# Two-layer decoder with experts: the expert weights' 16-bit halves prepared in an earlier phase, queries and keys saved in stacked order, another slot table for the routing

## The reference, cut to what matters

```python
x = x + L0_attn(ln(x))            # 16 heads of 16, full softmax, weights sign(W) * mean|W|
x = x + L0_xattn(ln(x), ctx)      # one head of 256, 64 context rows
x = x + L0_ffn(ln(x))             # ternary weights, 8-bit activations, 256 -> 1024 -> 256
x = x + L1_attn(ln(x))            # 16 heads: 4 causal, 12 causal with a window of 64
x = x + L1_xattn(ln(x), ctx, ctx) # 16 heads over 64 context rows
x = x + L1_ffn(ln(x)):            # 8 experts, the best 2 of each token, and a shared one
    shared = (silu(x @ sg.T) * (x @ su.T)) @ sd.T
    probs = sigmoid(x @ router.T + bias); top_p, top_i = top_k(probs, 2); top_p /= sum(top_p)
    for each expert e: y_e = (silu(x @ wg[e].T) * (x @ wu[e].T)) @ wd[e].T
    out = shared + sum over the two chosen of top_p * y_e
```

## Time and profile before

| | us |
|---|---|
| median of 3 runs | 2143.51 (2140.32 to 2156.59) |
| the profiled execution's own time | 2145.49 |
| its span, first to last instruction | 2143.4 |
| TensorE busy | 1688.7 (79%) |
| DVE / ACT / GpSimd busy | 1316.8 / 1118.9 / 979.4 |
| mean granted clock of TensorE | 0.889 |
| layer 0 attention | 0 to 586 |
| layer 0 cross-attention and feed-forward | 586 to 847 |
| layer 1 attention | 847 to 1352 |
| layer 1 cross-attention | 1352 to 1582 |
| experts: routing and shared expert | 1582 to 1762 |
| experts: blocks and end | 1762 to 2143 |

### The profile page before, as it was taken

One profiled execution on the slowest core, in us unless ns is written; L12 is line 12 of the kernel. 1 busy time (PEld: TensorE's weight loads), 2 busy tenths in 40 slices (PEclk: granted clock), 3 DMA queues, 4 the chain that ended last, 5 costly groups with the idle time before them and its releaser, 6 DMA issues. The chain is left out here.

```text
span 2143.4 us, 36053 instructions
## 1 busy us (share of the span) xinstructions
PE 1688.7 (79%) x12334; PEld 859.7 (40%) x12350; DVE 1316.8 (61%) x3599; ACT 1118.9 (52%) x1534; POOL 979.4 (46%) x987
## 2 busy tenths in 40 slices
PE   4888888888688887477777776577747779999997
PEld 2122222222245455123333333344424446666664
DVE  2666777777157897246666664455448865555555
ACT  2366676676445796245555554255446634444442
POOL 3144554541347630456777766255327751212222
PEclk8588999999789999669999988699968889999999
DMA  5331334330040000333333320322224432222216
GB/s 102 65 58 36 62 65 65 61 50 1 5 122 1 1 1 5 52 53 51 54 53 53 58 41 11 84 53 58 47 88 133 132 126 54 61 62 62 58 41 245
DMA packets 114435, 130.26 MB, mean 61 GB/s; under 512 B 22108, under 2 KB 98908, under 8 KB 114108
## 3 DMA queue, kind: packets, MB, share of 16 engines
q1 hardware_dynamic: 107780, 109.74, 25.0%
q0 software_dynamic: 6480, 18.23, 2.2%
HBM read 79.25 MB, written 47.55 MB: 59 GB/s over the span
## 5 line engine op out<-in xcount | busy, mean ns | idle before, releaser
L653 ACT ACTIVATE at_pexp<-ps 128x1024 f32<-128x1024 f32 (+3 forms) x480 | 385.8, 826 | 194.3 <-PE ps L890 193.1
L714 DVE TENSOR_REDUCE at_mx<-ps 128x1 f32<-128x512 f32 x512 | 324.2, 684 | 146.9 <-PE ps L897 144.9
L897 PE MATMUL ps<-at_ks,at_qs 48*128 48x512 f16 (+3 forms) x1024 | 288.7, 357 | 91.6 <-DVE at_mx L714 42.4
L161 PE MATMUL ps<-mo_wall,mo_xt 128*128 x1704 | 301.5, 327 | 1.0 <-DVE mo_xt L2540 0.5
L890 PE MATMUL ps<-at_qs,at_ks 50*128 50x512 f16 (+4 forms) x1024 | 249.7, 341 | 27.7 <-DMA at_qs<-at_mhl 23.1
L950 PE MATMUL ps<-at_pexp,at_vaug 128*32 128x512 f32 (+4 forms) x2048 | 223.4, 529 | 13.9 <-issue 11.2
L161 PEld LDWEIGHTS ps<-mo_wall,mo_xt 128*128 128x128 f16 x1704 | 161.2, 98 | 94.6 <-issue 3.5
L2304 POOL DMA_INDIRECT mo_yd<-mo_xn,mo_idu x71 | 68.1, 959 | 275.8 <-DVE mo_xn L2561 267.0
L716 DVE CUSTOM_DVE_ANT_0 at_junk<-ps,at_lmask 128x192 bf16<-128x192 f32 x384 | 115.5, 353 | 78.7 <-PE ps L897 77.5
L897 PEld LDWEIGHTS ps<-at_ks,at_qs 48*128 48x128 f16 x1024 | 75.6, 98 | 206.1 <-DVE at_mx L714 122.6
L2364 ACT ACTIVATE mo_sg<-ps 128x512 f32<-128x512 f32 x71 | 42.4, 597 | 186.9 <-PE ps L161 186.9
(11 more groups left out here) (396 smaller groups left out, 3853.2 us busy)
## 6 DMA issues: line engine op xcount, KB each, us to landing
at_qs<-at_scratch SPq DMA_DIRECT2D x96, 128.0 KB, 7.2
at_ks<-at_scratch SPq DMA_DIRECT2D x96, 128.0 KB, 7.8
mo_xw<-mo_xs SPq DMA_DIRECT2D x71, 136.0 KB, 2.4
at_scratch<-at_qkh SPq DMA_DIRECT2D x64, 128.0 KB, 1.8
at_scratch<-at_qkl SPq DMA_DIRECT2D x64, 128.0 KB, 1.8
mo_wall<-mo_yd SPq DMA_DIRECT2D x16, 512.0 KB, 10.8
x_qs<-x_queries SPq DMA_DIRECT2D x48, 128.0 KB
mo_stage<-in_m_gate SPq DMA_DIRECT2D x9, 512.0 KB, 3.9
```

The lines of the kernel that those rows point to most:

```text
L161: last = nc.tensor.matmul(out, lhs, rhs, start=(n == 0), stop=(n == len(terms) - 1))
L653: last = act.activation(columns(pexp[:, U % 2, hh], at, n, stride, width), columns(banks(r, ST[S % 2], 2), at, n, stride, width), ACT.Exp, ...
L714: last = ve.reduce_max(out, score, AX.X)
L897: return nc.tensor.matmul(banks(r, MX[i % 2])[:, piece.at:piece.at + piece.n], qs[rows, (n // 2) % 2, h // 2, piece.idx * P:(piece.idx + 1 ...
```

## The change

1. In layer 0 attention the side task grows from 12 chunks to 66: behind the 12 of `wlin` come 54 of the expert weights (9 experts x 3 matrices x 2 halves, 256 KB each). There are nine chunks per batch, at slots 1, 3, 5, 14, 15, 17, 28, 29 and 31 modulo 32. SP issues the load at the chunk's slot (behind the rows, saves, stack and x load of that slot), GpSimd does its three instructions one slot later, and SP stores the float16 halves (256 KB) to a DRAM tensor `moe_weights` four slots later.
2. `experts_phase` no longer loads float32 weights and no longer splits them. SP issues one DMA of 1.5 MB for the shared expert at the start and eight of 1.5 MB for the experts, each when the next batch's x is turned; the padding writes stand directly behind them.
3. `save` writes to DRAM in stacked order: three DMAs per piece in place of two (the half that the stack holds twice is written twice). `stack` then needs four DMAs of 48 partitions x 8 KB in place of twelve of 16 partitions. In layer 1 cross-attention it is six saves of 128 KB and two stack DMAs per batch.
4. `ROUTE` and `SHARED` get other slots, with the same periods; `SPLIT` goes.

```diff
+CHUNK_AT = (1, 3, 5, 14, 15, 17, 28, 29, 31)
+CHUNK_DO = (1, 1, 1, 4)
...
+            whalves = sb("whalves", [P, 2, 2, WCHUNK], F16)
...
-        scratch = nc.dram_tensor(f"{tag}_scratch", (nb, 2, P, 4, T), F16, kind="Internal").ap()
+        scratch = nc.dram_tensor(f"{tag}_scratch", (nb, 2, 2, 3 * DH, NP_, T), F16, kind="Internal").ap()
...
+        MOE_CHUNKS = 6 * (E_ + 1)
+        CHUNKS = LIN_CHUNKS + MOE_CHUNKS
+        def chunk_at(i):
+            return CHUNK_AT[i % len(CHUNK_AT)] + K * (i // len(CHUNK_AT))
...
             def save(b, m):
-                to = scratch[b] if b < nb else r.x1_queries[b - nb]
+                of_k, par = divmod(m, 2)
+                to = scratch[b, of_k, par] if b < nb else r.x1_queries[b - nb, par]
                 sp.wait_ge(qkh_ready, qk_before(b) + m + 1)
-                sp.dma_start(to[0, :, m, :], qkh[:, m, :]).then_inc(saved, 16)
+                for rep in (0, 1 + of_k):
+                    sp.dma_start(to[rep * DH:(rep + 1) * DH].rearrange("d i t -> i d t"), qkh[:, m, :]).then_inc(saved, 16)
                 sp.wait_ge(qkl_ready, qk_before(b) + m + 1)
-                sp.dma_start(to[1, :, m, :], qkl[:, m, :]).then_inc(saved, 16)
+                rep = 2 - of_k
+                sp.dma_start(to[rep * DH:(rep + 1) * DH].rearrange("d i t -> i d t"), qkl[:, m, :]).then_inc(saved, 16)
...
                 for par in range(2):
-                    for rep, (qpart, kpart) in enumerate(((0, 0), (0, 1), (1, 0))):
-                        rows = slice(64 * par + 16 * rep, 64 * par + 16 * rep + 16)
-                        sp.dma_start(qs[rows, p], scratch[b, qpart, :, par, :].rearrange("(i d) t -> d i t", d=DH)).then_inc(stacked, 16)
-                        sp.dma_start(ks[rows, p], scratch[b, kpart, :, 2 + par, :].rearrange("(i d) t -> d i t", d=DH)).then_inc(stacked, 16)
+                    rows = slice(64 * par, 64 * par + 3 * DH)
+                    for of_k, to in enumerate((qs, ks)):
+                        sp.dma_start(to[rows, p].rearrange("p i t -> p (i t)"), scratch[b, of_k, par].rearrange("p i t -> p (i t)")).then_inc(stacked, 16)
...
+            def keep_halves(j):
+                s, n, half = moe_chunk(j)
+                sp.wait_ge(lin_done, 2 * (LIN_CHUNKS + j + 1))
+                at = n * NW + half * WCHUNK
+                sp.dma_start(r.moe_weights[s, :, :, at:at + WCHUNK], whalves[:, j % 2]).then_inc(halves_out[j % 2], 16)
...
-                if binary and t >= 0 and t % (K // 2) == 4 and t // (K // 2) < LIN_CHUNKS:
-                    load_lin(t // (K // 2))
+                if binary:
+                    for i in chunks(t):
+                        load_lin(i)
+                    for i in chunks(t - CHUNK_DO[3]):
+                        if i >= LIN_CHUNKS:
+                            keep_halves(i - LIN_CHUNKS)
...
-                if binary and t >= K // 2 and t % (K // 2) == 4 and t // (K // 2) - 1 < LIN_CHUNKS:
-                    split_lin(t // (K // 2) - 1)
+                if binary:
+                    for i in chunks(t - CHUNK_DO[0]):
+                        scale_chunk(i)
+                    for i in chunks(t - CHUNK_DO[1]):
+                        chunk_high(i)
+                    for i in chunks(t - CHUNK_DO[2]):
+                        chunk_low(i)
...
-            for t in range(START, END):
-                for s, n in due(t, "LOAD"):
-                    load_weights(s, n)
-
+            sp.dma_start(sh[:].rearrange("p q n w -> p (q n w)"), r.moe_weights[0].rearrange("p q w -> p (q w)")).then_inc(sh_in, 16)
+            for e in range(E):
+                sp.wait_ge(xt_ready, 2 * (e + 1))
+                sp.dma_start(wall[:, e * EW:(e + 1) * EW], r.moe_weights[1 + e].rearrange("p q w -> p (q w)")).then_inc(wall_in, 16)
...
-ROUTE = {"STAT": -22, "RSTD": -17, "APPLY": -10, "HIGH": -10, "LOW": 2, "TURN": (-9, 6), "XT": (-3, 12), "LG": 6, "LOGITS": 17, "SIG": 16,
-         "CHOOSE": 20, "RANK": 18, "SLOTS": 27, "SCAT": (28, 30, 33, 49, 49, 49, 50, 51)}
+ROUTE = {"STAT": -22, "RSTD": -15, "APPLY": -11, "HIGH": -6, "LOW": 2, "TURN": (-14, 2), "XT": (0, 11), "LG": 3, "LOGITS": 16, "SIG": 18, "CHOOSE": 23,
+         "RANK": 16, "SLOTS": 28, "SCAT": (30, 31, 34, 43, 45, 46, 46, 49)}
-SHARED = {"GU": (11, 12, 41, 45), "SQ": (22, 33, 48, 50), "H": (26, 42, 49, 56), "HH": (38, 47, 48, 62), "HL": (43, 50, 66, 70), "PROJ": (64, 66),
-          "UPD": (77, 97)}
+SHARED = {"GU": (8, 9, 34, 41), "SQ": (27, 36, 47, 53), "H": (28, 38, 54, 56), "HH": (40, 40, 60, 63), "HL": (36, 47, 55, 56), "PROJ": (63, 65),
+          "UPD": (85, 99)}
-SPLIT = {"LOAD": (-105, -83, -71), "WHI": (-58, -42, -34), "WLO": (-42, -28, -19)}
-SPLIT_PERIOD = 35
```

More of the change, by code:

```diff
@@ L289, in attention_phase @@
             wstage = sb("wstage", [P, 2, WCHUNK])
+            whalves = sb("whalves", [P, 2, 2, WCHUNK], F16)
+            halves_out = [sem(f"halves_out{i}") for i in range(2)]
             x_in = [sem(f"x_in{b}") for b in range(nb)]
@@ L354, in attention_phase, with chunks, moe_chunk @@
         LIN_CHUNKS = NC * NLIN // WCHUNK
+        MOE_CHUNKS = 6 * (E_ + 1)
+        CHUNKS = LIN_CHUNKS + MOE_CHUNKS
+        def chunk_at(i):
+            return CHUNK_AT[i % len(CHUNK_AT)] + K * (i // len(CHUNK_AT))
+        def chunks(t):
+            return [i for i in range(CHUNKS) if chunk_at(i) == t]
+        def moe_chunk(j):
+            return j // 6, j % 6 // 2, j % 2
         def main_at(t):
@@ L439, in _ @@
                         load_x(b + 1)
-                if binary and t >= 0 and t % (K // 2) == 4 and t // (K // 2) < LIN_CHUNKS:
-                    load_lin(t // (K // 2))
+                if binary:
[5 more added lines that the diff above has]
+            if binary:
+                for i in range(2):
+                    sp.wait_ge(halves_out[i], 16 * MOE_CHUNKS // 2)
             if ahead:
-                sp.wait_ge(saved, 32 * qk_before(all_nb))
+                sp.wait_ge(saved, 48 * qk_before(all_nb))
         @block.gpsimd
@@ L1741, in save, with to @@
                 sp.wait_ge(q_ready, NC * (f + 1))
-                sp.dma_start(r.x1_queries[p, 0], qh[:]).then_inc(saved, 16)
+                def to(par, rep):
+                    return r.x1_queries[p, par, rep * DH:(rep + 1) * DH].rearrange("d i t -> i d t")
+                for par in range(2):
+                    for rep in range(2):
+                        sp.dma_start(to(par, rep), qh[:, par, :]).then_inc(saved, 16)
                 sp.wait_ge(ql_ready, f + 1)
-                sp.dma_start(r.x1_queries[p, 1], ql[:]).then_inc(saved, 16)
+                for par in range(2):
+                    sp.dma_start(to(par, 2), ql[:, par, :]).then_inc(saved, 16)
             def stack(b):
@@ L1755, in stack @@
                 if b >= AHEAD:
-                    sp.wait_ge(saved, 32 * (b - AHEAD + 1))
-                for rep, part in enumerate((0, 0, 1)):
-                    for par in range(2):
-                        at = 64 * par + 16 * rep
-                        sp.dma_start(qs[at:at + 16, p], r.x1_queries[p, part][:, par, :].rearrange("(i d) t -> d i t", d=DH)).then_inc(stacked[p], 16)
+                    sp.wait_ge(saved, 96 * (b - AHEAD + 1))
+                for par in range(2):
+                    sp.dma_start(qs[64 * par:64 * par + 3 * DH, p].rearrange("p i t -> p (i t)"), r.x1_queries[p, par].rearrange("p i t -> p (i t)")).then_inc(stacked[p], 16)
             def rows(b):
@@ L2311, in _ @@
         def _(act):
-            def split(s, n):
-                act.wait_ge(w_in[n], 16 * (s + 1))
-                act.activation(part_of(s, 0)[:, n * NW:(n + 1) * NW], stage[:, n, :], ACT.Copy, scale=WS).then_inc(w_hi, 1)
             def high(b):
@@ L2358, in _ @@
                     sigmoid(b)
-                for s, n in due(t, "WHI"):
-                    split(s, n)
             def block_squash(k):
@@ L2400, in settle @@
                 ve.wait_ge(step, steps.n)
-            def split(s, n):
-                ve.wait_ge(w_hi, 3 * s + n + 1)
-                part = slice(n * NW, (n + 1) * NW)
-                ve.scalar_tensor_tensor(out=part_of(s, 1)[:, part], in0=stage[:, n, :], scalar=WS, in1=part_of(s, 0)[:, part],
-                                        op0=ALU.mult, op1=ALU.subtract).then_inc(w_lo, 1)
             def apply(b):
@@ L2534, in _ @@
                         update(b, half).then_inc(x_done, 1)
-                for s, n in due(t, "WLO"):
-                    split(s, n)
             def block_in(k):
@@ L2669, in project @@
                     pe.wait_ge(y_ready, NK)
-                else:
+                elif b:
                     pe.wait_ge(x_done, 2 * (b - 1) + half + 1)
```

71 lines of the change are left out of this document (39 added, 32 removed).

## The result

The changed kernel takes 2168.9 us (median of 12 runs, 2157.2 to 2173.8) against 2142.6 us: ratio 1.0112, 95% interval 1.009 to 1.0133. The interval lies clear of 1: the kernel is slower by some 24 us by the ratio, 26 by the medians. Forecast was 2126, within 2090 to 2162. Its profiled execution spans 2169.6 us, 26.2 more than before.

The account below looks back on a forecast made before the run. TensorE was taken to set layer 0's pace, DVE to be routing's nearest bound. From 2145.5 us, experts -31.5, stacks -12.7 and layer 0 +25 gave 2126.3, so 2126, within 2090 to 2162.

Parts of the forecast that it names:

- Layer 0: Layer 0 attention: 54 more chunks on GpSimd make the split of the maxima late, +25 us, bounds 0 to +55.
- That is 2.1 late at best ... Sum 4.4 us late: Layer 0, slot 28 to the slot-11 split: 2.1 us late, +2 behind the stack, +0.3 for loads under chunks.
- Six batches have such a stretch; the last has no stack in it (2.5): Layer 0 count of late stretches: five at 4.4 us plus a last at 2.5, 24.5 us, taken as +25.
- Stacks: First stacks of three attention phases: four 48-partition DMAs at 170 GB/s come sooner, -12.7 us, from -2 to -22.
- that comes back, with the time to its last issue: Awaited first stacks: 4.6 us less transfer plus issue time saved; layer 0 -5.7, layer 1 -5, cross-attention only -2.
- Experts: Routing part of the experts: float32 loads and splits go, gaining at start, middle and end, -31.5 us in sum.
- Start: Routing start: without old splits and their waits, statistics follow the router at once, -6.5 us, between -3 and -7.
- end: Routing end: pads no longer stand behind the last weight load, so sorted rows are read sooner, -7 us, -4 to -10.
- The middle: Routing window: 22 DVE splits, 27.9 us, go; DVE 85% busy, so two thirds are gained, -18 us.
- New slots at nothing: Routing tables: new slots issue the same work in another order and cost nothing beyond the other terms.
- The third: Rival in layer 0: GpSimd becomes the bound behind stacks still at 113 GB/s, +55, total 2167 us; chance 0.13.
- The first: Rival in layer 0: the chunks fit GpSimd's idle time, costing 5 us or less, total 2104 us; chance 0.25.

Follow-up runs that it names:

- loads-ahead side task: Changed kernel with the chunks' loads and stores moved ahead of saves and stack on SP, one chunk of nine moved on GpSimd: 2126.9 us, ratio 0.9941 to the kernel before.

## Why the prediction was wrong

**What bounds the kernel** was right for layer 0: the split of the maxima is TensorE's wait, and GpSimd's busy share says little.

**Layer 0, +25 forecast, +49.6 measured in the wait.** The step that failed is "That is 2.1 late at best ... Sum 4.4 us late", and the count behind it. The mechanism was right, its size was half of what came. The fifth stretch, which has no load of x, is 7.3 late:
- the first chunk starts 426.60 - 416.25 = 10.35 us after the split at slot 28, not 398.2 - 389.3 = 8.9: its load is issued 0.3 us later, behind the third save, and lands after 3.8 us for 2.7. +1.4;
- a chunk back to back is 2.97, not 2.87: +0.6 for six;
- the wait behind the stack is 3.0, not 2: +1.0. The 0.3 for two waits did not come.

With 4.4 these give 7.1. Where x is loaded, SP issues 512 KB ahead of the chunk, which the prediction left out though it named SP's queue: 2 us more of idle, some 1.5 of lateness.

"Six batches have such a stretch; the last has no stack in it (2.5)" is a miscount. Seven stretches hold six chunks, and six of them have a stack; the seventh, without one, costs nothing in the wait. From split to split the six are 2.8, 8.7, 9.0, 8.9, 7.3 and 11.2 us longer than before, together 226.6 - 178.8 = 48 us, for 5 x 4.4 + 2.5. The average, 8.0, lies in the range given for a stretch, 0 to 9, and the last lies outside it. Nearly all of these errors had the same sign: it was a sum of things that just fit, and where a chain has no slack, an omitted term only makes it longer.

**Stacks, -12.7 forecast, -7.3 at the three starts** (-3.4, -3.0 and -0.9 where TensorE resumes, against the phase's start). The rate was nearly right, 162 GB/s over the 8 us that the stack of layer 1 fills, up to 172, for the 170 taken:

```profile
931.00:933.00 2.00, 0.00 (x0) 0.00 (x0) 0.00 (x0) 0.00 (x0) 1.86 (x2) 0.83 1.11 172
931.00:939.00 8.00, 1.03 (x8) 0.77 (x8) 0.00 (x0) 1.02 (x1) 4.20 (x3) 0.58 1.03 162
```

What failed is "that comes back, with the time to its last issue": in layer 1 the stack went from issue to TensorE in 11.8 us for 15.5, 3.7 less, so the issues had been under the transfer; and it starts 0.7 us later, since SP waits 2.3 us for the last save's landing, where before it waited 1.4.

An estimate from the Trainium skill's port rule ("SBUF — State Buffer", Door 1) gave 9.6 us for the stack without its start and landing, and 1.57 MB at 162 GB/s are 9.7: here the trace agrees. The Trainium skill's rule on dividing dimensions ("DMA: Bandwidth & Descriptors", "Why a DMA increments its semaphore by 16 and not by 1") spoke for slower saves, and the stack did wait those 2.3 us for 1.4, but no run separates that rule from the third DMA.

**Experts, -31.5 forecast, -21.0 between the two profiles and -24 by the median of twelve.** Start (-5.5 for -6.5) and end (-6.5 for -7) were right; the gap at the end was shown alone as well. The middle failed: -10.3, or -13 by the median, for -18. The step is "DVE is 85% busy, so nearer the first end ... I take two thirds". Work put back on DVE in the deleted instructions' form makes the same stretch 8 us (new slots) or 12 (old slots) longer for 34 us of work: a quarter to a third, where two thirds were taken. That is most of the 10 to 13 us gained there; what ACT's casts and the waits on loads add was not tried. With the splits gone DVE is busy 99 of 146 us and TensorE 116 (79%); what sets the pace then wasn't shown. New slots at nothing was right with the splits gone; with splits in place they gain 5.6 us in the part, so they can't be priced without saying which kernel they stand in.

**The rivals.** The third had the time, 2167, by luck. Its cause did not hold: the stack ran at 162 GB/s, not 113. The lateness that it needed, over 5.6 us a stretch, was there (8.0), but it was made up of the late first loads, the load of x and the wait behind the stack; and the routing gave less than it assumed (21 for 31.5), the stacks more (7.3 for 2). The first, that the chunks fit, is what they do once their loads stand elsewhere.

## What to carry to other kernels

When work is added to an engine that has room, lay out the stretch between two things that others wait for, with its loads: where each load stands in its queue, behind which transfer, and which buffer it waits for. If it just fits, take the price as one-sided, because every term that was forgotten adds to it. And read where an engine is idle while it is late: two waits in a row hide each other, so move both loads, not the one with the longer wait.

## What was not expected of the hardware

With most of the work taken out, the loads alone made TensorE wait 2.2 to 5.8 us for the split in each stretch from slot 28 to slot 11: a 256 KB load landed 8.5 us after its issue behind the 1.5 MB stack of the changed kernel and 10.9 in that experiment, for 2.7 with a free queue.

The same code in layer 0, that of the loads-ahead side task, ended at 586.7, 587.0, 587.9, 596.7 and 597.8 us in five profiles. TensorE's wait for the split, in that order 15.4, 22.2, 17.6, 21.3 and 19.3 us, doesn't explain it. The granted clock over the whole phase goes with it: 0.94, 0.90 and 0.90 in the three shorter ones, 0.88 in the two longer. The kernel that ended at 587.9, and the one that ended at 597.8:

```profile
0.00:587.90 587.90, 478.60 (x2844) 142.97 (x2844) 373.21 (x679) 344.29 (x393) 385.17 (x438) 0.90 0.41 107
500.00:600.00 100.00, 72.69 (x413) 22.29 (x411) 37.46 (x76) 47.99 (x55) 46.82 (x55) 0.81 0.18 56
```

```profile
0.00:597.80 597.80, 486.63 (x2844) 145.32 (x2844) 373.71 (x679) 344.84 (x393) 385.35 (x439) 0.88 0.40 105
500.00:600.00 100.00, 75.44 (x452) 22.88 (x444) 43.23 (x84) 53.98 (x61) 44.35 (x54) 0.86 0.11 35
```

The clock of the last batch alone says nothing: from 500 to 600 us the longer of the two has the higher one. Why one execution is granted more than another wasn't tried, and five profiles are few. A phase's length in a single profile says no more than some 10 us here, and waits and gaps say more.
